# Windowed linear attention in a convolution block: an earlier release for the pooled kv convolution, VectorE's turns behind both divisions, and another order at the start and the end

## The reference, cut to what matters

```python
xw = x.reshape(B, C, Hn, ws, Wn, ws)...            # windows of 4 x 4, ws = 4
qkv = jnp.einsum('nchw,oc->nohw', xw, qkv_w)       # 3 x 128 channels
pooled = _avg_pool5(qkv)                           # 5 x 5 mean inside the window
msq = jnp.concatenate([qkv, pooled], axis=1)       # heads of 8 channels, full and pooled
q = relu(msq[..., :8]); k = relu(msq[..., 8:16]); v = msq[..., 16:]
v = jnp.pad(v, ..., constant_values=1.0)           # a ninth column of ones
kv = jnp.einsum('ngld,nglm->ngdm', k, v)
out = jnp.einsum('ngld,ngdm->nglm', q, kv)
out = out[..., :-1] / (out[..., -1:] + 1e-15)
y = jnp.einsum('nchw,oc->nohw', out, proj_w)       # 256 -> 128 channels
y = y * inv + shift                                # batch norm, inv and shift per channel
return x + y
```

## Time and profile before

| | |
|---|---|
| median of 3 runs | 846.03 us (845.71 to 847.62) |
| the profiled execution | 847.76 us, span 846.0 us |
| PE busy | 800.9 us, 95% |
| PEld busy | 659.3 us, 78% |
| DVE busy | 639.7 us, 76% |
| POOL busy | 592.1 us, 70% |
| ACT busy | 571.7 us, 68% |

### The profile page before, as it was taken

One profiled execution on the slowest core, in us unless ns is written; L12 is line 12 of the kernel. 1 busy time (PEld: TensorE's weight loads), 2 busy tenths in 40 slices (PEclk: granted clock), 3 DMA queues, 4 the chain that ended last, 5 costly groups with the idle time before them and its releaser, 6 DMA issues. The chain is left out here.

```text
span 846.0 us, 62390 instructions
## 1 busy us (share of the span) xinstructions
PE 800.9 (95%) x28226; PEld 659.3 (78%) x28226; DVE 639.7 (76%) x1249; ACT 571.7 (68%) x1350; POOL 592.1 (70%) x1336
## 2 busy tenths in 40 slices
PE   0779999999999999999999999999999999999996
PEld 0568888888878888888888887888788888888884
DVE  7647787887777888888676878888776767676776
ACT  0456767677676767676767767676767676777764
POOL 0456777777777777777777777777777777777771
PEclk9999999999999999999999999999999999999999
DMA  7012221000022222000011212100000000000001
GB/s 283 2 32 73 67 84 38 29 19 29 19 65 60 80 67 73 29 19 28 20 46 56 84 56 84 39 27 28 19 29 19 29 19 28 19 28 19 28 19 39
DMA packets 20642, 38.73 MB, mean 46 GB/s; under 512 B 2416, under 2 KB 15216, under 8 KB 20592
## 3 DMA queue, kind: packets, MB, share of 16 engines
q1 hardware_dynamic: 20592, 38.25, 14.0%
HBM read 19.36 MB, written 18.87 MB: 45 GB/s over the span
## 5 line engine op out<-in xcount | busy, mean ns | idle before, releaser
L383 ACT ACTIVATE q_full<-ps,cst 128x384 f32<-128x384 f32 x192 | 103.5, 590 | 228.7 <-PE ps L683 228.7
L288 POOL TENSOR_TENSOR xd<-x_all,mean_t 128x384 f32<-128x384 f32 x95 | 78.7, 829 | 182.4 <-PE ps L690 163.0
L663 PE MATMUL ps<-wkv_sb,xn 128*128 128x256 f32 x576 | 144.6, 388 | 21.9 <-DVE xn L516 21.9
L266 POOL TENSOR_TENSOR x_all<-y_pool,x_all 128x96 f32<-128x96 f32 x380 | 148.3, 425 | 13.8 <-ACT y_pool L405 13.8
L663 PEld LDWEIGHTS ps<-wkv_sb,xn 128*128 128x128 f32 x576 | 103.5, 193 | 32.3 <-issue 21.9
L565 DVE TENSOR_TENSOR x_all<-ps,x_all 128x384 f32<-128x384 f32 x96 | 53.5, 557 | 93.3 <-PE ps L771 93.1
L364 ACT ACTIVATE vm_pool<-ps,cst 128x256 f32<-128x256 f32 x288 | 119.2, 521 | 0.0
L672 PE MATMUL ps<-wkv_sb,xp 128*128 128x256 f32 x384 | 107.1, 401 | 9.5 <-ACT q_pool L383 2.2
L714 PEld LDWEIGHTS ps<-kvc_full,q_full 64*32 64x32 f32 x9216 | 88.0, 106 | 27.3 <-issue 27.3
L364 ACT ACTIVATE vm_full<-ps,cst 128x384 f32<-128x384 f32 x192 | 101.1, 578 | 9.1 <-PE ps L702 2.5
L672 PEld LDWEIGHTS ps<-wkv_sb,xp 128*128 128x128 f32 x384 | 65.0, 189 | 51.7 <-issue 25.1
(11 more groups left out here) (71 smaller groups left out, 1418.0 us busy)
## 6 DMA issues: line engine op xcount, KB each, us to landing
out<-x_all SPq DMA_DIRECT2D x96, 192.0 KB, 1.9
x_all<-x SPq DMA_DIRECT2D x36, 384.0 KB, 3.3
x_all<-x SPq DMA_DIRECT2D x6, 768.0 KB, 7.8
wkv_sb<-wkv SPq DMA_DIRECT2D x1, 128.0 KB, 10.7
wq_sb<-wq SPq DMA_DIRECT2D x1, 128.0 KB, 10.5
proj_sb<-proj SPq DMA_DIRECT2D x1, 128.0 KB, 10.2
cst<-consts SPq DMA_DIRECT2D x1, 90.0 KB, 10.8
bn_sb<-bn SPq DMA_DIRECT2D x1, 2.0 KB, 10.2
```

What stands on the lines that cost most here:

```text
L266: return pool.tensor_tensor(o, a, b, ALU.add)
L288: link(pool.tensor_tensor(xd[:], x_all[:, s * SP:(s + 1) * SP], mean, ALU.subtract), 1)
L383: return act.activation(to, src, ACT.Relu, scale=col(mask))
L663: last = pe.matmul(ps[:, bank, at:at + 2 * P], xn[:, p, t * P:(t + 1) * P], wkv_sb[:], start=True, stop=True)
```

## The change

It has four parts. (1) `conv_kv_pooled` waits for `qm_f` (the full q's copy) instead of `qm_p`; the wait for `qm_p` stands in `out_wait`, and so before the pooled projection. (2) VectorE's `divide` is split into `divide` and `turn`: both divisions first, then both turns; each multiplication has one more wait, for the turn of the strip before. The averages over the groups of an image are spread over five strips instead of four. (3) At the start, strip 0 has its full q in bank 5 (`Q_F_FIRST`) and its q convolution, full and pooled, and first kv products in front of the kv convolution of strip 1; the projection weights are turned last. The ones in the v tiles are set before the batch norm's scale, ScalarE's second square root comes behind the first k, and `projT` is copied inside VectorE's first step. (4) At the end, the last strip's pooled out products stand in front of the pooled projection of strip 94, and VectorE adds strip 94's full projection behind all of strip 95's divisions and turns.

```diff
@@ relu_q (ScalarE)
+                bank = Q_F_FIRST if is_first(s) else Q_F
@@ ScalarE, start
             square_root(0)
-            square_root(1)
...
             masked_v_full(0)
             relu_k(0)
+            square_root(1)
+            relu_q(0)
             relu_k_pooled(0)
             masked_v_pooled(0)
+            relu_q_pooled(0)
@@ VectorE, divide and turn
+                wait(dve, turned, s)
                 dve.tensor_tensor(o[:].rearrange("p n (h m) -> p (n h) m", m=D), src[:, :, 0:D],
                                   den[:].unsqueeze(2).to_broadcast([P, HALF * 4, D]), ALU.mult).then_inc(done, 1)
+
+            def turn(s, pooled):
...
@@ VectorE, step
-                if is_last(s):
-                    divide(s, False)
-                if not is_first(s):
+                if not is_first(s) and not is_last(s):
+                    residual(s - 1)
+                divide(s, False)
+                if is_last(s):
+                    turn(s, False)
+                divide(s, True)
+                if not is_last(s):
+                    turn(s, False)
+                turn(s, True)
+                if is_last(s):
                     residual(s - 1)
-                if not is_last(s):
-                    divide(s, False)
-                divide(s, True)
@@ TensorE, conv_kv_pooled and out_wait
-                wait(pe, qm_p, s)
+                wait(pe, qm_f, s)
...
                     pe.wait_ge(kvc_p, s + 1)
+                    pe.wait_ge(qm_p, s + 1)
@@ TensorE, start
             conv_kv(0, 0)
+            conv_q_full(0, 0)
             conv_kv_pooled(0, 0)
-
+            conv_q_pooled(0, 0)
+            pe.wait_ge(ones_set, 1)
+            kv_products(0)
+            conv_kv(1, 1)
+            kv_products_pooled(0)
+            conv_kv_pooled(1, 1)
             pe.wait_ge(proj_scaled, 1)
+            pe.wait_ge(kvc_f, 1)
             for z in range(2):
                 last = pe.transpose(ps[:, PROJ_T, z * P:(z + 1) * P], proj_sb[:, z * P:(z + 1) * P], col(C_IDENT, P))
             last.then_inc(proj_turned, 1)
-            conv_kv(1, 1)
-            pe.wait_ge(projT_ready, 1)
-            pe.wait_ge(ones_set, 1)
-            kv_products(0)
-            kv_products_pooled(0)
-            conv_q(0, 0)
@@ TensorE, end
             out_products(NS - 1)
-            project(NS - 2)
+            project_full(NS - 2)
             out_products_pooled(NS - 1)
+            project_pooled(NS - 2)
             project(NS - 1)
```

More of the change, by code:

```diff
@@ L93, in build @@
     GROUPING = 3 + 2 * FOURS
[L94 removed]
+    assert FOURS * 4 == SPB and GROUPING + 5 < SPB and (SPB + 3 - GROUPING) % 2 == 0
     x_v = x.rearrange("b c h w -> c b (h w)")
@@ L218, in over_strips @@
                 at = t * 2 if s >= 3 and b + 1 < B and t < 2 * FOURS else None
-                phase = t - 2 * FOURS if s >= 3 and b + 1 < B and 0 <= t - 2 * FOURS < 4 else None
+                phase = t - 2 * FOURS if s >= 3 and b + 1 < B and 0 <= t - 2 * FOURS < 5 else None
                 step(s, b + 1, at, phase)
@@ L417, in step @@
             def step(s, b, at, phase):
-                relu_q(s)
-                relu_q_pooled(s)
+                if not is_first(s):
+                    relu_q(s)
+                    relu_q_pooled(s)
                 if not is_first(s) and not is_last(s):
@@ L582, in divide @@
             def divide(s, pooled):
-                ready, done, free, turned, bank, den, o, o_t, step = (
-                    (out_p, num_p, y_p, turned_p, OUTP, den_pool, o_pool, o_pool_t, 2) if pooled else
-                    (out_f, num_f, y_f, turned_f, OUTF_LAST if is_last(s) else OUTF, den_full, o_full, o_full_t, 0))
+                ready, done, turned, bank, den, o, step = (
+                    (out_p, num_p, turned_p, OUTP, den_pool, o_pool, 2) if pooled else
+                    (out_f, num_f, turned_f, OUTF_LAST if is_last(s) else OUTF, den_full, o_full, 0))
                 dve.wait_ge(ready, s + 1)
@@ L589, in divide @@
                 link(dve.reciprocal(den[:], den[:]), s, step + 2)
+                wait(dve, turned, s)
                 dve.tensor_tensor(o[:].rearrange("p n (h m) -> p (n h) m", m=D), src[:, :, 0:D],
                                   den[:].unsqueeze(2).to_broadcast([P, HALF * 4, D]), ALU.mult).then_inc(done, 1)
+            def turn(s, pooled):
+                done, free, turned, o, o_t = (
+                    (num_p, y_p, turned_p, o_pool, o_pool_t) if pooled else (num_f, y_f, turned_f, o_full, o_full_t))
                 dve.wait_ge(done, s + 1)
@@ L636, in _ @@
             dve.tensor_scalar(proj_sb[:], proj_sb[:], bn_inv[:], None, ALU.mult).then_inc(proj_scaled, 1)
[L638 to L645, removed]
-            dve.tensor_copy(projT[:], ps[:, PROJ_T, 0:2 * P]).then_inc(projT_ready, 1)
             over_strips(step)
@@ L676, in conv_q, with conv_q_full, conv_q_pooled @@
             def conv_q(s, p):
-                full = xn[:, p].rearrange("p (a r x) -> p r a x", r=PAIR, x=PX)
+                conv_q_full(s, p)
+                conv_q_pooled(s, p)
+            def conv_q_full(s, p):
+                if is_first(s):
+                    pe.wait_ge(bank_zero, 1)
+                bank = Q_F_FIRST if is_first(s) else Q_F
+                full = xn[:, p].rearrange("p (a r x) -> p r a x", r=PAIR, x=PX)
+                for r in range(PAIR):
+                    last = pe.matmul(ps[:, bank, PX + r * SP // PAIR:PX + (r + 1) * SP // PAIR], wq_sb[:, r], full[:, r],
+                                     start=True, stop=True)
+                last.then_inc(q_f, 1)
+            def conv_q_pooled(s, p):
                 pooled = xp[:, p].rearrange("p (q j) -> p q j", j=H64)[:, :, 0:WIN_H * PXP].rearrange(
                     "p q (a r x) -> p r q a x", r=PAIR, x=PXP)
-                for r in range(PAIR):
-                    last = pe.matmul(ps[:, Q_F, PX + r * SP // PAIR:PX + (r + 1) * SP // PAIR], wq_sb[:, r], full[:, r],
-                                     start=True, stop=True)
-                last.then_inc(q_f, 1)
-                if isinstance(s, int) and s == 0:
-                    pe.wait_ge(bank_zero, 1)
                 wait(pe, num_p, s)
@@ L762, in out_products_pooled, with project_full @@
                 out_products_of(q_pool, kvc_pool, OUTP, EP).then_inc(out_p, 1)
-            def project(s, out_next=False):
+            def project_full(s):
                 pe.wait_ge(turned_f, s + 1)
@@ L779, in project @@
                           start=True, stop=True).then_inc(y_p, 1)
+            def project(s, out_next=False):
+                project_full(s)
+                project_pooled(s, out_next)
             def step(s, p):
@@ L784, in step @@
                     conv_kv(s + 1, p)
-                conv_kv_pooled(s + 1, p)
-                if not is_first(s):
+                    conv_kv_pooled(s + 1, p)
                     project(s - 1, out_next=True)
```

28 lines of the change are left out of this document (22 added, 6 removed).

## The result

| | before | after |
|---|---|---|
| median of the runs | 846.57 us (845.71 to 847.62, 4 runs) | 805.18 us (803.98 to 807.73, 4 runs) |
| profiled execution, its span | 847.76, 846.0 | 805.22, 803.4 |

The ratio is 0.9515, interval 0.9489 to 0.954: 41 us faster. The forecast was 805.0.

A forecast was written before the change was run, and what follows sets the result against it. TensorE, busy 132.36 of 133.40 us, was taken as the bound. Steady part 38 + start 4.5 - end 1.9 = 40.6 us, from 847.76 to 807.2, or 805.4 at the median, rounded to 805; range 798 to 822.

The forecast's parts named there:

- The wait of L672: Pooled kv convolution's weight loads: waiting only for the full q's copy saves 0.31 us in 94 strips, 29 us.
- rival 2: Pooled kv convolution held by something else: 820 if half the waits stay, 834 if all; chance 0.28 together with rival 1.
- The wait of L690: Pooled q convolution behind VectorE's pooled multiplication: moving the turns last saves 0.11 us in 92 strips, 10 us.
- (a): ScalarE's chain up to the pooled v, before L702's load: cover shrinks from 0.50 us; some 0.1 left after the release.
- rival 1: ScalarE's chain replaces the wait, costing 0.1 to 0.25 us per strip: 814 to 828; chance 0.28 together with rival 2.
- (b): VectorE's pooled own-heads product before the load of L777, the pooled projection: cover shrinks from 0.91 to 0.49 us.
- (c): A batch's averages spread over five strips: three strips each may delay the residual a little; 1 us allowed in all.
- Rival 3: Late VectorE turns delay the next own-heads products: decides from 0.9 us added; 862 us at 1.1; chance 0.04.
- The start: Before the loop, bounded by ScalarE: first out products at about 33.5 instead of 37.50; gain 4.5 us, bounds 0 and 5.5.
- The end: Last strips: strip 94's residual waits behind the last strip's pooled turn; cost 1.9 us, bounds 0 and 2.5.
- The fetch: TensorE's 1.06 us pause before the 68 remaining pooled out products: if it belongs to the place, it stays.
- The rival of 810: Pause before the remaining pooled out products: a fetch paced by time gives back the head's 4.5 us; no separate chance.

The follow-up runs named there:

- experiment 1: Kernel before with only the release changed: pooled kv convolution waits for the full q's copy, pooled projection for the pooled q's; 816.53 us, ratio 0.9629.
- 2: Kernel before with only VectorE's turns moved behind both divisions, plus a wait for a turn before each multiplication; 847.54 us, ratio 0.9993.
- 8: Kernel before with the release changed and the turns behind both divisions, start and end as before; 805.22 us, ratio 0.951.
- 5: Kernel after with one more ScalarE operation per strip, a 128-column copy into a spare tile ahead of the pooled v; 822.49 us, ratio 0.9707.
- 6: Kernel after with two spare VectorE turns per strip behind the pooled turn; 813.68 us, ratio 0.9603.
- 12: Kernel after with three spare VectorE turns per strip into spare tiles; 854.83 us, ratio 1.0089 against the kernel before.
- 3: Kernel before with the new start alone, including strip 1's changed release there and averages over five strips; 843.7 us, ratio 0.9953.
- 9 to 11: Three versions rerun on one chip: kernel after 805.75 us; kernel before with release and turns changed 805.91; kernel after with its end undone 803.54.
- both_steady_again: Rerun of the kernel before with release and turns changed, old start and end; 805.91 us, ratio 0.9508.
- 4: Kernel after with only its end undone, both TensorE's order and VectorE's residual of strip 94; 804.26 us, ratio 0.9489.
- 7: Kernel after with VectorE's residual of strip 94 back between the last strip's divisions, TensorE's new end kept; 804.7 us, ratio 0.9488.
- tail_back_again: Rerun of the kernel after with only its end undone; 803.54 us, ratio 0.9482.

## Why the prediction was right, step by step

- **The wait of L672: right.** Predicted 29 us, L663 to L771 at 2.16 to 2.2; measured 29.1 in the strips (31 with what it gives at the start, experiment 1), and 2.18. The doubt over the strips without a named releaser (rival 2) is settled: both strips of the pair lost their wait, 0.34 and 0.29 us.
- **The wait of L690: right in the sum, but only beside the other edit.** Predicted 10 us; it is 0 alone (2) and 11 behind the release (8). The sum treated the two as independent terms. They are not, since the gate of L672 is timed from the same q convolution. The prediction took them together, where it didn't matter; had it priced the turns alone by the same row, it would have been wrong by 10 us.
- **The covers.** (a) was 0.1 in the prediction and is 0.02 at most (5), since the release of that load takes 0.12, not the 0.05 that I took from another place (in the earlier trace rows L672's load starts 0.11 behind the copy, so a longer one was on view). The forecast held by luck of hundredths: with 0.1 us less of cover the strips would have cost 94 x 0.08 = 7.5 us more (an estimate), rival 1 in small. (b) was 0.49 and is 0.86 to 0.91 (6, 12), for two reasons of like size: I counted to the load and not to the matmul (0.2 with the release), and the pooled own-heads product ends sooner behind the full q convolution's start than I had it, 403.41 - 400.44 = 2.97 us where it was 410.48 - 407.25 = 3.23, with the two turns now back to back (408.38, 408.87). (c) allowed 1 us for the averages; in the kernel after no strip from 75 us on is 0.1 us off the mean, so they cost nothing. The steady part as a whole was put at 38 us and measured 40.
- **Rival 3's size: wrong, by cover (b).** A strip was to be longer than before from 0.9 us of added time on, but 0.91 us made it 7.96 (8.34 before), and only 1.38 us made it 8.42. By the measured cover the point is 0.86 + 0.43 = 1.29 us, and the 1.1 us behind the 862 would have given some 828 (estimates).
- **The start.** Predicted a gain of 4.5; the loop begins 4.15 sooner in the profiled pair, and the start alone gave 4.0 us (3). With the new loop about 2.4 are left (9 to 11). Two things are seen. The sum took the start and the release as separate terms, but 0.7 us belong to both. And the prediction read one execution's clock as a property of the old start: its second kv convolution, 2.77 us in the earlier trace rows, at a granted 0.50, took 1.51 at 1.00 in both_steady_again. What remains of the difference is not settled; the last section has what is known.
- **The end.** Predicted 1.9 us lost; measured 2.04 in the trace and 2.2 by medians. The named step, the residual behind the last strip's pooled turn, is the cause (4, 7). It is a loss, and leaving it out is the better kernel. Two small parts I did not have nearly cancel: the pooled out products end 0.31 us sooner behind the first out product (794.91 - 790.75 = 4.16, where it was 839.80 - 835.33 = 4.47), and after 2.48 us of idle the last full projection ran partly at the lower clock level (granted 0.67 on average from 797.96 to 799.17; it took 1.21 us where it took 0.91 at 1.00 before).
- **The fetch.** Predicted to stay with its place: it does. With one projection fewer ahead of the pooled out products, 29 of their matmul records come before the pause; with both ahead (4) 27 do: 96 + 2 + 29 and 96 + 4 + 27 are both 127 records behind the loop's exit; in the kernel before it is 96 + 4 + 28 = 128. (These are the "128 products" of the prediction: records, two to an fp32 product, and each has a weight load.) The Trainium skill, Advanced Engine Details and Errata, section ISA Cache, has 256 instructions in a line. The trace agrees with a boundary there: 127 or 128 weight loads and as many matmuls are 254 or 256 instructions. That the pause is a fetch is not shown. The rival of 810, a fetch paced by time, did not come: the whole gain of the start would have been lost, and 4.0 us of it (3) and 2.4 (9 to 11) were measured.

## What to carry to other kernels

Follow a wait to the event that times it: two waits in a row that hang on one event are not two terms, and the saving at the first is waited for at the second until that one is released. Look as well for the same gate outside the loop: here the release alone also shortened the start. Count a cover on TensorE to the start of the matmul that needs the operand, not to its early weight load, and take the release from a row at that very place. Read the granted clock beside every time that is taken from a start or an end, and take more than one execution. At the end of a program put an operation that others hang on into the first free stretch of its engine; moved behind the last strip's work it lengthened the end by 2 us.

## What the hardware showed besides

TensorE pauses without a releaser at the same places of the program in every version (near the start behind 346, 599 and 852 matmul records with the new start, behind 347, 600 and 853 with the old one), but the pause's length changes from execution to execution of the same instructions: at the end it is 1.06 us in the kernel before, and this in the version both_steady, whose end is the same:

```profile
795.23 0.45 PE L724 MATMUL ps<-kvc_pool,q_pool 64*32 64x36 f32 x28
796.27 0.80 PE L724 MATMUL ps<-kvc_pool,q_pool 64*32 64x36 f32 x68 [0.59 <-issue]
```

Behind such pauses the granted clock falls to the lower level (1.2 GHz) for a while in some executions and not in others; a mean below 1.00 is a mixture of both levels. The stretch from 45 to 75 us (columns as in the earlier trace rows), in the kernel after:

```profile
45.00:75.00 30.00, 25.93 (x903) 22.76 (x906) 19.31 (x38) 17.66 (x43) 18.56 (x44) 0.94 0.21 61
```

in tail_back, which has the same instructions there:

```profile
45.00:75.00 30.00, 25.88 (x961) 22.65 (x961) 20.85 (x42) 17.95 (x43) 20.18 (x47) 1.00 0.22 61
```

and in residual_early, too:

```profile
45.00:75.00 30.00, 25.64 (x731) 22.41 (x733) 18.14 (x35) 15.77 (x38) 16.86 (x38) 0.89 0.21 61
```

Granted 1.00, 0.94 and 0.89, the loop's first three strips took 28.39, 30.01 and 31.95 us. So up to 3.6 us of a start's gain or loss is up to this. For tail_back_again I had expected some 30.0 us at 0.94: it was granted 0.94 and took 30.57, so the pauses' lengths count beside the clock.

The stretch ahead of the loop has the same trouble. From 28 to 44 us, in the kernel before and in both_steady_again, with the same columns:

```profile
28.00:44.00 16.00, 12.58 (x382) 10.55 (x383) 8.37 (x19) 8.32 (x21) 4.76 (x11) 0.89 0.01 3
28.00:44.00 16.00, 12.97 (x391) 11.26 (x392) 8.48 (x19) 10.30 (x25) 6.55 (x13) 1.00 0.01 3
```

With the old start the loop begins at 43.50 to 43.96 us in the three profiles granted 0.89 here (before, turns_only, both_steady), and at 42.89 and 41.74 in the two granted 1.00 (release_only, both_steady_again). With the new start it begins at 39.38 to 39.67 in five granted 1.00, and at 40.71 in tail_back_again, granted 0.89; with spare operations it was as late as 43.82 (scalar_longer, granted 0.79, with one more pause of 2.47 us). So the 4.15 us between the two profiles compare a start at 0.89 with one at 1.00. At 1.00 on both sides and with the release in both it is 2.1 to 3.5 us, which fits the 2.4 us by medians.

Too few profiles were taken to say whether the new start meets the lower clock more or less often than the old one. The loop's fourth kv convolution started at 68.02 to 71.33 us in five profiles with the new start and the new loop (mean 69.98), and at 71.56 and 71.87 in the two with the old start and the new loop, a difference of 1.7 us.
